# Feed-forward blocks taken between cross-attention tiles, their layer norms and routing lagged into later tiles

## What is computed

```
y = layernorm(y + attention(y, y, y, causal=True), g1, beta1)
y = layernorm(y + attention(y, Z, Z, causal=False), g2, beta2)
h = relu(y @ w1 + b1)
y = layernorm(y + h @ w2 + b2, g3, beta3)
x = x + y
h = _layernorm(x)
top-2 of softmax(h @ wg.T) -> expert_w
x = x + sum over experts of expert_w * (silu(h @ w1[e]) * (h @ w3[e])) @ w2[e]
```

## Time and profile before

| | |
|---|---|
| median of 3 runs | 641.57 us (639.85 to 641.93) |
| the profiled execution | 642.41 us, its span 640.5 us |
| PE busy | 554.9 us, 87% of the span |
| PE weight loads | 376.9 us, 59% |
| DVE busy | 389.2 us, 61% |
| ACT busy | 283.9 us, 44% |
| POOL busy | 260.3 us, 41% |

### The profile page before, as it was taken

One profiled execution on the slowest core, in us unless ns is written; L12 is line 12 of the kernel. 1 busy time (PEld: TensorE's weight loads), 2 busy tenths in 40 slices (PEclk: granted clock), 3 DMA queues, 4 the chain that ended last, 5 costly groups with the idle time before them and its releaser, 6 DMA issues. The chain is left out here.

```text
span 640.5 us, 12727 instructions
## 1 busy us (share of the span) xinstructions
PE 554.9 (87%) x4132; PEld 376.9 (59%) x4133; DVE 389.2 (61%) x1005; ACT 283.9 (44%) x569; POOL 260.3 (41%) x288
## 2 busy tenths in 40 slices
PE   3897999999999999997989668385893999999993
PEld 2564756677767777674565535243562666666662
DVE  4899684487787777769798468452442434343432
ACT  2765655445546455465457144222341223232321
POOL 4357140042313223127142706226445656566643
PEclk9999999999999999999899969698897999999997
DMA  7134321022011111110143811215423344333323
GB/s 238 34 93 123 107 77 50 1 71 95 34 65 35 63 65 34 34 34 17 42 140 100 58 23 46 49 50 41 57 39 25 55 64 58 58 57 57 58 41 34
DMA packets 34903, 38.81 MB, mean 61 GB/s; under 512 B 9741, under 2 KB 26190, under 8 KB 34862
## 3 DMA queue, kind: packets, MB, share of 16 engines
q1 hardware_dynamic: 26350, 28.00, 17.3%
q0 software_dynamic: 8512, 10.26, 11.2%
HBM read 28.23 MB, written 10.02 MB: 60 GB/s over the span
## 5 line engine op out<-in xcount | busy, mean ns | idle before, releaser
L874 PE MATMUL ps<-arena,tT 128*128 x936 | 164.7, 333 | 5.1 <-ACT tT L693 2.9
L874 PEld LDWEIGHTS ps<-arena,tT 128*128 128x128 f16 x936 | 91.2, 100 | 62.3 <-issue 11.1
L1667 DVE SCALAR_TENSOR_TENSOR w1m<-ps,w1m 128x512 f32<-128x512 f32 x39 | 27.0, 692 | 101.2 <-ACT w1m L833 91.5
L833 ACT ACTIVATE w1m<-ps 128x512 f32<-128x512 f32 x39 | 23.3, 597 | 136.0 <-PE ps L874 79.1
L662 POOL DMA_INDIRECT out<-y,qst x39 | 61.9, 1588 | 45.1 <-issue 18.9
L874 PE MATMUL ps<-arena,probT 128*128 128x256 f16 (+1 forms) x624 | 73.9, 272 | 0.2 <-DVE probT L1418 0.2
L874 PE MATMUL ps<-arena,qT 128*128 128x512 f16 (+1 forms) x384 | 70.7, 333 | 0.0
L874 PEld LDWEIGHTS ps<-arena,probT 128*128 128x128 f16 (+1 forms) x624 | 59.6, 97 | 7.9 <-DVE probT L1418 0.4
L693 ACT ACTIVATE probT<-ps 128x512 f16<-128x512 f32 (+1 forms) x80 | 43.2, 572 | 44.3 <-PE ps L977 39.5
L693 ACT ACTIVATE tT<-ps 128x512 f16<-128x512 f32 (+1 forms) x86 | 46.9, 597 | 27.8 <-PE ps L1133 14.8
L874 PE MATMUL ps<-tT 128*128 128x512 f16 (+3 forms) x240 | 52.9, 361 | 5.5 <-DVE probT L1338 3.5
(11 more groups left out here) (175 smaller groups left out, 963.1 us busy)
## 6 DMA issues: line engine op xcount, KB each, us to landing
stage<-we_in SPq DMA_DIRECT2D x44, 256.0 KB, 2.6
y<-x_in SPq DMA_DIRECT2D x4, 512.0 KB, 5.7
xin<-x_in SPq DMA_DIRECT2D x4, 512.0 KB, 5.4
out<-y SPq DMA_DIRECT2D x4, 512.0 KB, 3.3
hrow<-probT SPq DMA_DIRECT2D x4, 512.0 KB, 9.3
stage<-z_in SPq DMA_DIRECT2D x4, 256.0 KB, 5.4
prob<-w_in SPq DMA_DIRECT2D x4, 256.0 KB, 3.6
stage<-w_in SPq DMA_DIRECT2D x4, 256.0 KB, 2.8
```

The lines of the kernel that those rows point to most:

```text
L833: a.activation(sil[:, q, :], ps[2 * q][:], ACT.Silu, scale=1.0 / WS).then_inc(sm["e_sil"], 1)
L874: r = t.matmul(o, lhs(a), rhs(b), start=first and n == 0, stop=last and n == 2)
L1667: v.scalar_tensor_tensor(act[:, q, :], ps[2 * q + 1][:], 1.0 / WS, sil[:, q, :], ALU.mult, ALU.mult).then_inc(sm["e_act"], 1)
```

## The change

- The feed-forward is cut into five units: blocks 0, 1 and 2 whole, block 3 in two halves of 256 tokens. Units 0, 1 and 2 are taken after cross tiles 5, 9 and 13, unit 3 after tile 15, unit 4 last. The loops over cross tiles are written out.
- In a unit, the down of chunk f-2 follows the up of chunk f. Ups have three banks, ReLU writes its second result into its bank and `hid_lo` reads it there. A down adds to all tokens of the unit in banks 4 to 7. The scores of the next cross tile stand between the last downs.
- Statistics, `centre` and the routing end of the block before follow a unit on DVE; `first_out`, `x1_stats` and `x1_aggr` come after the next tile, `h_norm` before the one after it, `h_lo` one later. `h_trans` and `logits` are in the next unit, the scatter of a block behind it.
- The 13 weight pieces: five on ACT and DVE between tile 15 and unit 3, eight among the odd chunks of units 3 and 4. On SP, nine record loads stand between the five and the eight.
- In the experts, block 2's scatter stands before gather 4, block 3's h, logits and ranks two tiles later than before.

```diff
-        RANKS2_AT, H_AT, LOGITS_AT, RANKS_AT = 2, 4, 6, 8
+        UNITS = ((0, 0, TB), (1, 0, TB), (2, 0, TB), (3, 0, 2), (3, 2, 2))
+        AFTER = {5: 0, 9: 1, 13: 2, NT - 1: 3}
+        FIRST = {5: 0, 9: 1, 13: 2}
+        R15 = 5
+        H_AT, LOGITS_AT, RANKS_AT = 6, 8, 10
...
 sync
-            for j in range(NB):
-                if j:
-                    store_x1(sp, j - 1)
...
-                split_ff(split_load, sp, j)
-                if j:
-                    store_h(sp, j - 1)
+            for m in range(R15):
+                split_rest(split_load, sp, m)
+            store_x1(sp, 2)
             load_recs(0)
+            for m in range(R15, len(rest)):
+                split_rest(split_load, sp, m)
+                if m == R15 + 2:
+                    store_h(sp, 2)
...
 gpsimd
-            gather(0)
-            gather(1)
+            for n in range(4):
+                gather(n)
+            recs_loaded(0)
+            scatter(NB - 2, range(TB))
             rstd_of("n_", NB - 1)
-            gather(2)
-            rstd_of("m_", NB - 1)
-            gather(3)
             for n in range(NJ):
-                for j, at in ((NB - 2, RANKS2_AT), (NB - 1, RANKS_AT)):
+                if n == 2:
+                    rstd_of("m_", NB - 1)
+                if n == RANKS_AT - 1:
+                    recs_loaded(1)
+                    scatter(NB - 1, range(TB))
...
 scalar
+            def ffn(u):
+                j = UNITS[u][0]
+                for f in range(KF):
+                    relu(u, f)
+                    if u in (1, 2) and f in (3, 4):
+                        h_copy(j - 1, f - 3)
+                    if u > 2 and f % 2:
+                        rest_hi(R15 + (u - 3) * 4 + f // 2)
+                    if u == 3 and f == 1:
+                        h_hi(2)
+                    if u == 3 and f in (6, 7):
+                        h_copy(2, f - 6)
...
+                split_cross(split_hi, act_, i)
+                if last:
+                    for m in range(R15):
+                        rest_hi(m)
+                ffn(u)
+                if not last:
+                    if u:
+                        gates(u - 1)
+                    for c in range(C_CH):
+                        c_exps(i + 1, 1 - q, c)
...
 tensor
+                c_trans(i, q, 0)
+                c_trans(i, q, 1)
+                y_trans(u, i)
+                c_pv(i, q, 0)
+                c_trans(i, q, 2)
+                c_pv(i, q, 1)
+                c_trans(i, q, 3)
...
+                up(u, 0)
+                up(u, 1)
+                c_pv(i, q, 2)
+                c_pv(i, q, 3)
+                if last:
+                    break
+                up(u, 2)
+                down(u, 0, i)
+                up(u, 3)
+                if u:
+                    h_trans(u - 1, 0)
+                down(u, 1, i)
+                up(u, 4)
...
+                up(u, 7)
...
+                c_scores(i + 1, 1 - q, (0,))
+                down(u, 5, i)
+                c_scores(i + 1, 1 - q, (1,))
+                down(u, 6, i)
+                c_scores(i + 1, 1 - q, (2, 3))
+                down(u, 7, i)
...
 vector
+            for i in range(NT):
+                q = i % 2
+                if i not in AFTER:
+                    if i - 2 in FIRST:
+                        h_norm(FIRST[i - 2])
+                    c_step(i, q, i + 2 < NT)
+                    if i - 1 in FIRST:
+                        j = FIRST[i - 1]
+                        first_out(j)
+                        x1_stats(j)
+                        x1_aggr(j)
+                    if i == 14:
+                        table_starts(0)
+                        table(0)
+                    if i - 3 in FIRST:
+                        h_lo(FIRST[i - 3])
+                    continue
+                un, last = AFTER[i], i == NT - 1
+                if last:
+                    h_norm(2)
+                c_los(i, q, 0)
+                c_los(i, q, 1)
+                y_lo(un)
...
+                for f in range(3, KF):
+                    hid_lo(un, f)
+                    if un and f == 5:
+                        choose(un - 1)
+                if un:
+                    place_read(un - 1)
...
+                for c in range(C_CH):
+                    c_max(i + 1, 1 - q, c)
+                c_bias(i + 1, 1 - q)
+                for m in range(TB):
+                    out_tile(un, m)
+                moments(un)
+                centre(un)
+                if un:
+                    routed(un - 1)
```

More of the change, by code:

```diff
@@ L426, in _ @@
                 load_x(b, "x2_in")
[L427 to L430, removed]
+            for s in range(2, NT):
                 split_cross(split_load, sp, s)
+                if s in (8, 12):
+                    store_x1(sp, s // 4 - 2)
+                    load_x(s // 4, "x2_in")
+                if s in (9, 13):
+                    store_h(sp, s // 4 - 2)
             def load_rec(n, q):
@@ new lines, in _ @@
+            for i in range(NT):
+                if i not in AFTER:
+                    c_step(i, i % 2, True, i + 2 < NT)
+                    if i - 2 in FIRST and i < NT - 1:
+                        h_hi(FIRST[i - 2])
+                    continue
+                q, u, last = i % 2, AFTER[i], i == NT - 1
+                c_his(i, q, 0)
+                c_his(i, q, 1)
+                y_hi(u)
+                c_his(i, q, 2)
+                c_his(i, q, 3, not last)
+                if not last:
+                    q_hi(i + 2, q, psT[1])
+                split_cross(split_hi, act_, i)
[3 more added lines that the diff above has]
+                ffn(u)
+                if not last:
+                    if u:
+                        gates(u - 1)
+                    for c in range(C_CH):
+                        c_exps(i + 1, 1 - q, c)
@@ L903, in c_scores @@
                 for c in cs:
+                    if not first and i - 1 in FIRST:
+                        if c < 3:
+                            wait(pe, "f_lo", KF * FIRST[i - 1] + 6 + c)
+                        elif FIRST[i - 1]:
+                            wait(pe, "r_rk", FIRST[i - 1])
+                            if FIRST[i - 1] > 1:
+                                wait(pe, "r_used", FIRST[i - 1] - 1)
                     if first:
@@ new lines, in _ @@
+            for f in range(3, KF):
+                hid_lo(3, f)
+                if f == 3:
+                    h_lo(2)
+                if f % 2:
+                    split_rest(split_lo, dve, R15 + f // 2 - 1)
+            y_lo(4)
+            split_rest(split_lo, dve, R15 + 3)
+            for m in range(2):
+                out_tile(NB - 1, m)
+            for f in range(KF):
+                hid_lo(4, f)
+                if f == 1:
+                    choose(2)
+                if f == 6:
+                    place_read(2)
+                    table_counts(1)
+                if f % 2:
+                    split_rest(split_lo, dve, R15 + 4 + f // 2)
@@ L1665, in gated @@
+            for m in range(2, TB):
+                out_tile(NB - 1, m)
+            routed(NB - 2)
             def gated(n, q):
@@ L1693, in _ @@
             gated(0, 0)
-            x1_stats(j)
+            moments(j)
             gated(1, 1)
-            x1_aggr(j)
+            centre(j)
             act_lo(0, 0)
```

557 lines of the change are left out of this document (278 added, 279 removed).

## The result

The changed kernel takes 661.02 us (median of 4 runs, 658.50 to 662.39) where the kernel before took 641.75 (4 runs, 639.85 to 642.67) on the same chip: a ratio of 1.030, with a 95% interval of 1.026 to 1.034. It is 3% slower. The forecast was 659 (640 to 672), slower at 0.76.

The account below looks back on a forecast made before the run. PE bounds the cross stage and has waits only in the feed-forward. Cross stage with three blocks, joins and clock 391, then work and waits to experts at 440.6, plus 217.5: span 658.1, forecast 659 us (640 to 672).

Parts of the forecast that it names:

- Joins: Cross stage, where units meet tiles: VectorE work ahead of c_los(0) makes PE wait, 5.2 us at tiles 7 and 11, 33.2 in all.
- Tile 15: Start of tile 15: block 2's first_out, stats and aggregate, the table and h_norm ahead of c_los cost PE 9.0 us.
- The unit's own tiles 9 and 13: c_los(0) is wanted 1.8 us after tile start and h_lo stands before it: 1.6 us lost at each.
- The ends of the units: VectorE's statistics, centre and routing ahead of c_los(0): 2.2 us lost, 3.9 each for units 1 and 2.
- Unit 3: After tile 15: PE waits 7.5 us for weight pieces through two stage buffers, then 10.4 for piece 5 behind record loads.
- the second half's 2.6 and 0.5: Unit 3: piece 7 behind relu 5 costs h_trans' second half 2.6 us, the y and h chain 0.5.
- Experts start: PE's first expert work starts at 440.6 us, where it started at 413.70; the rest falls from 226.8 to 217.5.
- gather 4: Expert stage: block 2's scatter stands before gather 4, so PE waits 5.6 us, with 1.8 for the clock.
- 1.8 us on each wait of over 5 us: Clock loss behind waits at tiles 7, 11, 15 and unit 3's second; half on two of nearly 4: 9.0 us.
- Absorbed: Rival, cross stage: VectorE's idle 2.5 us per tile takes the added work, joins cost nothing: 629 us, chance 0.16.
- SyncE's order is harmless: Rival, unit 3: record loads finish early or piece 5 is loaded before, 10.4 + 1.8 less: 647 us, chance 0.15.
- Gathers late: Rival: the record scatter after the units makes loads and gathers land late, 10 to 15 more: 672 us, chance 0.09.

Follow-up runs that it names:

- the trace without the stop: The kernel before, unchanged, taken again on another chip: median 641.59 us, ratio 1.001 to the kernel before.
- the spread version: Changed kernel with blocks 0 and 1's first outputs, statistics, aggregate and layer norm moved to places where VectorE idles or the next unit: 646.15 us, ratio 1.017.
- eight slots: Changed kernel with eight stage buffers for the weight pieces of units 3 and 4, eight loads issued before the record loads: 636.49 us, ratio 1.000.
- six ahead: Changed kernel with gather 4 before block 2's record scatter and every later gather one tile earlier: 648.52 us, ratio 1.019.
- combined edits: Changed kernel with spread VectorE work, table inside tile 14, eight stage buffers, earlier gathers and GpSimd's vector wait moved later: 620.88 us, ratio 0.979.
- block 2's norm in unit 3: Changed kernel with all five edits, and block 2's first output, statistics and layer norm in unit 3 instead of ahead of tile 15: 626.88 us, ratio 0.989.

## Why the prediction was right, point by point

**Right, by its steps.** Joins: 5.2 at tiles 7 and 11, measured 4.74 and 4.87, and the run with 1.4 us more work shows that nothing behind c_los absorbs any of it. Tile 15: 9.0, measured 8.44. The unit's own tiles 9 and 13: 1.6 each, measured 1.26 and 0.66. The ends of the units: 2.2 and twice 3.9. PE's brackets there are smaller (1.35, 2.80 and 2.94), but from the last down to the start of the next tile it takes 2.0, 3.5 and 3.6 us more than a steady tile (209.50 to 221.51, 284.23 to 297.68, 359.95 to 373.32, against 10.00, 10.00 and 9.78), since the first transposes also take 1.30 us in place of 1.04 there. Unit 3: 7.5 and 10.4, measured 8.62 and 11.41; with the second half's 2.6 and 0.5, 21.1 against 21.7. ScalarE did wait for piece 5's load behind the record loads, as the order of SyncE's queue had said. Experts start: 440.6, measured 441.50; from there to the end 217.5, measured 217.5, with a wait of 4.16 for gather 4 (5.6 predicted) and 9.87 at block 3 (9.78). The scatter of block 2 takes 443.35 to 453.43, 10.1 us, as summed. hid_lo from PSUM is no slower: its 24 passes of 512 columns average 690 ns, 879 in the earlier trace rows.

**Mis-sized, and luck.** The total is closer than its parts. From tile 5's start to tile 15's last transposes the sum has 215.2 us, the trace 210.3 (177.50 to 387.76): 4.9 too much, most of it in the joins, which are each a little too high. (The listed 5.7 for unit 2 and tile 13 also is 5.5 by its terms, 3.9 and 1.6.) From there to the experts' first ups the sum has 49.6, the trace 53.7: 4.1 too little. Of that 1.7 are the clock: the prediction puts 1.8 us on each wait of over 5 us but leaves out unit 3's first, and behind the waits of 8.62 and 11.41 us the same matmuls take 1.4 and 2.1 us more than at full clock; another 1.1 us is PE's idle time before 441.50. And the tiles started 1.64 later than summed (177.50, not 175.86). These three cancel to 0.9 us, which is luck. In the cross stage the clock's price came out at 3.1 for tile 7, 2.5 for tile 11 (297.68 to 315.05, 17.37, less 10.00 and 4.87) and 1.3 for tile 15, where 1.8 each was put, and nothing behind the ends of units 1 and 2, where 0.9 each was put (their waits are 0.70 and 2.10 to 2.24 with work between): 1.8 was read from 12 matmuls, and behind tile 7's wait 24 matmuls and the transposes ran slower.

**Misread.** The prediction puts the 3.10 us at 441.28 of the earlier trace rows down to the record scatter. That row says "issue", and ScalarE stood in an unnamed stop there. The sum is not hurt, since the trace without the stop has 10.76 in place of 3.10 and 6.99.

**Missed.** GpSimd's wait for the vectors, moved ahead of the first cross tile by the change, costs 1.56 us at 144.25, as the run without it shows. The prediction started its sum at tile 5 and took what is before as unchanged; what is queued behind a moved wait has to be asked at each place the diff touches, small or not.

**The rivals.** "Absorbed" falls with the run that added passes; but it names something real, since the spread version gets VectorE's idle time for the same work. "SyncE's order is harmless" falls with the trace, 11.41 us behind the record loads, and with the wait that followed them when they were moved; loads ahead of them, with eight slots, gain 21.7 us on both waits of unit 3. "Gathers late" falls, as PE waited for them about as long as summed; six ahead takes 9.7 us of that away. The Trainium skill (TensorE: Matmul & The Clock Gate, HAM oscillation) warns of waits that let the clock fall again and again; the trace agrees, with granted clocks of 0.50 behind tile 7's wait of 4.74 and 1.00 behind unit 3's of 1.51.

## What to carry to other kernels

Price what is moved in an in-order queue by the slack of the operation right behind it, and not by the engine's idle share: 75% busy VectorE had none where the work was put, and enough a few operations on. Before adding a phase to a queue, list the long things that share it (nine record loads of 1.3 us each on SyncE, with two slots behind them, stood behind 20 us of PE's waits here), and give the consumer buffers enough to be ahead of them; another order alone left the time where it was. Then measure combined edits too: here they added in stretches that have separate waits (36.8 of 38.6 us), and 9 of 11 us were missing in the expert stage, where other waits lay beside the one removed. Last, taking a wait away can uncover another that it had hidden: read the row again before the next theory.

## What the hardware showed that was not expected

- A VectorE operation with both inputs in SBUF takes up to three times as long beside GpSimd's 128x1024 additions. In the changed kernel a weight-piece low takes 2.17 us at 419.63, and 0.69 elsewhere, while GpSimd runs its addition from 418.58 to 421.26:

```profile
419.63 2.17 DVE L304 SCALAR_TENSOR_TENSOR arena<-stage,arena 128x512 f16<-128x512 f32 x1
...
418.58 2.68 POOL L604 TENSOR_TENSOR xin<-xin,vec 128x1024 f32<-128x1024 f32 x1
```

  The Trainium skill (SBUF — State Buffer, Who interferes with whom) says that such an operation contends with a GpSimd one that reads SBUF, the shared ports being an exclusive lock; the rows agree: the low ends at 421.80, 0.54 us after GpSimd's. It names tensor_scalar too as able to take the shared ports, which is the operation of the four passes of 4.36 us in the kernel with block 2's norm in unit 3. That they met the same lock is argued, not shown.
- The clock was at 0.50 behind tile 7's wait of 4.74 us, and the tile lost 3.1 us, two thirds of the wait again. A longer wait did not cost more: 1.4 us behind 8.62, 2.1 behind 11.41, 1.3 behind 8.44, each with other work behind it.
- Nine loads of 1 KB with addresses from registers took 11.4 to 12.0 us of SyncE in every trace, about 1.3 us each, whatever ran beside them. What sets the price was not tested.
- The unnamed stops of ScalarE (10.46 us in one trace, 11.26 in another) come and go with one and the same kernel: one of the two traces of the kernel before has them. Eleven of over 3.5 us stand in four traces, in the cross stage too, and each begins while GpSimd issues the eight parts of a record scatter: the one of 4.61 us begins at 357.90, the scatter beside it is issued from 350.99 to 360.89. The other traces have the same scatters and no stop, so the scatter alone doesn't make one. They remain unexplained.
